# Projection with the first and second halves of all heads as two row tiles: rotary products without a rotation matmul

## The reference

```python
def rope(Y):                      # d = 16, so halves of 8
    ...
    Y2 = jnp.concatenate([-Y[..., d // 2:], Y[..., :d // 2]], axis=-1)
    return Y * cos + Y2 * sin     # cos, sin: the same 8 angles for both halves
q = split_heads(x @ Wq.T + bq); k = split_heads(x @ Wk.T + bk); v = split_heads(x @ Wv.T + bv)
q, k = (rope(q), rope(k))
att = softmax(causal(q k^T / sqrt(16)))
x = layernorm(x + (att @ v) @ Wo.T + bo)
x = layernorm(x + ffn(x))         # four ternary linear layers of width 1024, silu and gelu
```

## Time and profile before

| | |
|---|---|
| median of three runs | 2792.42 us (2791.34 to 2792.55) |
| profiled execution | 2795.36 us, span 2793.6 us |
| granted TensorE clock, mean | 0.989 of full |
| busy share of the span | PE 98%, DVE 68%, ACT 48%, POOL 5% |
| projection | 5.5 to 133.4 us of the span |

### The profile page before, as it was taken

The page is one execution under the profiler, slowest core; times in us unless marked ns, Lnnn a source line. Parts: engine busy times, 40 slices in busy tenths (PEclk is TensorE's granted clock), DMA queues, the critical chain, the costliest instruction groups (busy, mean ns, idle before and its releaser), DMA issues.

```text
span 2793.6 us, 39368 instructions
## 1 busy us (share of the span) xinstructions
PE 2729.1 (98%) x14880; PEld 1424.9 (51%) x14880; DVE 1899.9 (68%) x4003; ACT 1348.4 (48%) x2641; POOL 138.3 (5%) x206
## 2 busy tenths in 40 slices
PE   8899999999999999999999999999999999999998
PEld 4423333333333333333323333588888887888887
DVE  6999999888888888888887774633333352443343
ACT  4436666777776777777777776411111111000100
POOL 3300110001100001100000000000000000000000
PEclk9979999999999999999999999999999999999999
DMA  7731110001110011110001000411111132121100
GB/s 217 204 74 39 30 30 26 3 15 32 29 43 6 5 33 32 30 34 3 1 3 39 19 5 9 118 58 58 58 58 58 43 128 108 46 82 54 45 16 23
DMA packets 95613, 133.47 MB, mean 48 GB/s; under 512 B 31462, under 2 KB 69094, under 8 KB 91718
## 3 DMA queue, kind: packets, MB, share of 16 engines
q1 hardware_dynamic: 81452, 96.25, 10.7%
q0 software_dynamic: 6336, 23.34, 3.8%
q10 hardware_dynamic: 7648, 11.54, 1.5%
HBM read 83.77 MB, written 47.32 MB: 47 GB/s over the span
## 4 chain that ended last, share of the span: by engine, by line
PE 88%; DVE 6%; issue 2%; ACT 1%; DMA 1%; SPq 0%; ACTq 0%; POOLq 0%; POOL 0%; DVEq 0%
PE wi_f L984 19%; PE at_o L533 18%; PE at_row L498 17%; PE at_key L512 16%; PE na_h L1202 13%; PE na_y L1214 3%; DVE at_segmax L584 3%; DVE fr_masked L580 1%; DMA values<-pr_vals 1%; ACT at_probs L648 1%; PE at_key L515 1%; PE wi_p L833 1%; DVE pr_parts L252 0%; DVE pr_full L248 0%; PE pr_main L130 0%
## 5 line engine op out<-in xcount | busy, mean ns | idle before, releaser
L648 ACT ACTIVATE at_probs<-at_key 128x512 f32<-128x512 f32 (+3 forms) x2304 | 1127.3, 567 | 502.4 <-PE at_key L512 353.2
L584 DVE TENSOR_REDUCE at_segmax<-at_row 128x1 f32<-128x512 f32 x1792 | 1142.8, 684 | 169.2 <-PE at_row L498 164.9
L512 PE MATMUL at_key<-fr_q_stack,fr_k_stack 99*128 99x512 bf16 (+3 forms) x1152 | 415.0, 365 | 1.3 <-ACT at_probs L648 1.0
L498 PE MATMUL at_row<-fr_k_stack,fr_q_stack 96*128 96x512 bf16 (+3 forms) x1152 | 404.6, 376 | 10.8 <-DVE at_mask L612 5.5
L498 PE MATMUL at_row<-at_k_stack,at_q_stack 96*128 96x512 bf16 (+3 forms) x1152 | 408.1, 364 | 1.8 <-DVE at_segmax L584 1.1
L512 PE MATMUL at_key<-at_q_stack,at_k_stack 99*128 99x512 bf16 (+3 forms) x1152 | 402.2, 364 | 7.5 <-ACT at_probs L648 6.9
L1202 PE MATMUL na_h<-fr_h,fr_h2w_h 128*128 128x512 f32 x1024 | 322.1, 396 | 1.4 <-DVE fr_h L730 1.4
L533 PE MATMUL at_o<-at_probs,fr_values 128*32 128x512 f32 (+3 forms) x2304 | 289.0, 574 | 0.0
L533 PE MATMUL at_o<-at_probs,at_values 128*32 128x512 f32 (+3 forms) x2304 | 287.9, 572 | 0.0
L580 DVE CUSTOM_DVE_ANT_0 fr_masked<-at_row,fr_causal 128x384 f32<-128x384 f32 (+3 forms) x512 | 243.8, 483 | 45.1 <-PE at_row L498 44.7
L498 PEld LDWEIGHTS at_row<-fr_k_stack,fr_q_stack 96*128 96x128 bf16 x1152 | 110.3, 99 | 308.3 <-DVE at_segmax L584 160.1
(11 more groups left out here) (121 smaller groups left out, 2558.1 us busy)
## 6 DMA issues: line engine op xcount, KB each, us to landing
hidden<-wi_h SPq DMA_DIRECT2D x64, 256.0 KB, 2.0
na_h2f<-hidden SPq DMA_DIRECT2D x8, 1024.0 KB, 7.7
q_parts<-pr_parts SPq DMA_DIRECT2D x48, 128.0 KB, 2.4
k_parts<-pr_parts SPq DMA_DIRECT2D x48, 128.0 KB, 3.3
at_q_stack<-q_parts POOLq DMA_DIRECT2D x48, 128.0 KB, 3.5
at_k_stack<-k_parts POOLq DMA_DIRECT2D x48, 128.0 KB, 3.8
values<-pr_vals SPq DMA_DIRECT2D x32, 136.0 KB, 3.3
outputs<-at_outs SPq DMA_DIRECT2D x128, 34.0 KB
```

The costliest lines, as they stand in the source:

```text
L498: last = nc.tensor.matmul(bank[:, 0:w], qst[u][0:SROWS, c, h, i * P:(i + 1) * P], kst[u][0:SROWS, h, s * CH:s * CH + w], start=True, stop= ...
L512: last = nc.tensor.matmul(bank[:, q0:CH], kst[u][0:SROWS + PARTS, h, j * P:(j + 1) * P], qst[u][0:SROWS + PARTS, c, h, q0:CH], start=True, ...
L584: nc.vector.tensor_reduce(segmax[:, n % 2, h * TPC + i, s:s + 1], row_ps[r % RING_R][:, 0:w], op=ALU.max, axis=AX.X).then_inc(rows_taken, 1)
L648: nc.scalar.activation(probs[:, g % RING_P, h, q0:CH], key_ps[m % RING_K][:, q0:CH], ACT.Exp).then_inc(probs_ready, 1)
```

## The change

The rows of Wq and Wk and their biases are reordered on the way in: all first halves of the 16 heads (16 x 8 = 128 rows) are one tile, all second halves the other. A unit is now a **pair** of these tiles, q or k: g = 2n + m, 16 pairs. `rope` then works within partitions: full[first] = t1[first] - t2[second], full[second] = t1[second] + t2[first], with t2 = `lin` x sin. The matrix `turn`, `rotate` and `rot_ps` go. Four banks take the main products. Two `linear`, two POOL products and two sums are made per pair, 512 wide each; t2, rest, parts and ACT's two parts operations are made once per pair, 1024 wide. t2 reads `lin` in SBUF, where L237 read PSUM. The three parts of a half are stored by one DMA of 384 KB, so two DMAs a pair. `load_first` for the early chunks moves from ACT's queue to SP's, ahead of SP's wait for the parts. PE in `attend` waits for `consts_ready` only at the first turned row tile, and for `v_taken` only at the first keys; `t2_ready` isn't waited for any more.

```diff
-    UNITS = 2 * DH
-    NU = UNITS * NCH
+    PAIRS = 2
+    NU = PAIRS * NCH
     BUFS = 3
-    SLOTS = 4
+    SLOTS = 3
...
-            main(0)
             for g in range(NU):
-                if g + 1 < NU:
-                    main(g + 1)
-                rotate(g)
-                if g % 2 == 1:
-                    values(g // UNITS, g % UNITS // 2)
+                main(g)
+                values(*divmod(g, PAIRS))
...
+                m = g % PAIRS
+                for half in range(2):
+                    act.wait_ge(main_ready, 2 * g + half + 1)
+                    if g >= 2:
+                        act.wait_ge(t1_ready, 2 * (g - 2) + half + 1)
+                        act.wait_ge(t2_ready, g - 1)
+                    nc.scalar.activation(lin[:, g % 2, half, :], main_ps[2 * (g % 2) + half][:, :], ACT.Identity,
+                                         bias=bias[:, 2 * m + half:2 * m + half + 1],
+                                         scale=HD ** -0.5 if m == 0 else 1.0).then_inc(lin_ready, 1)
...
-                if 2 <= n < 2 + FIRST_EARLY:
-                    if m == 0:
-                        for slot in range(SLOTS):
-                            act.wait_ge(parts_stored[slot], 16 * PARTS * (n - 1))
-                    front.load_first(act, qp_d, kp_d, n - 2, range(m, len(TERMS), UNITS))
...
+                for half in range(2):
+                    pool.wait_ge(lin_ready, 2 * g + half + 1)
+                    if g >= 2:
+                        pool.wait_ge(full_ready, 2 * (g - 2) + half + 1)
+                    nc.gpsimd.tensor_tensor(t1[:, g % 2, half, :], lin[:, g % 2, half, :], cos[:, n % BUFS, :], ALU.mult
+                                            ).then_inc(t1_ready, 1)
...
-                    dve.wait_ge(rot_ready, g + 1)
-                    nc.vector.tensor_tensor(t2[:, g % 2, :], rot_ps[g % 2][:, :], sin[:, n % BUFS, :], ALU.mult
+                    dve.wait_ge(lin_ready, 2 * g + 2)
+                    if g >= 1:
+                        dve.wait_ge(full_ready, 2 * g)
+                    nc.vector.tensor_tensor(t2[:, :, :], lin[:, g % 2, :, :],
+                                            sin[:, n % BUFS, :].unsqueeze(1).broadcast_to([P, 2, CH]), ALU.mult
                                             ).then_inc(t2_ready, 1)
...
+                    for half, op in enumerate((ALU.subtract, ALU.add)):
+                        dve.wait_ge(t1_ready, 2 * g + half + 1)
+                        nc.vector.tensor_tensor(full[:, g % 2, half, :], t1[:, g % 2, half, :], t2[:, 1 - half, :], op
+                                                ).then_inc(full_ready, 1)
                 if 2 <= g:
                     dve.wait_ge(mid_ready, g - 1)
...
+                    nc.vector.tensor_tensor(parts[:, (g - 2) % SLOTS, 2, :, :], rest[:, (g - 2) % 2, :, :],
+                                            parts[:, (g - 2) % SLOTS, 1, :, :], ALU.subtract).then_inc(parts_ready, 1)
+                if g < NU:
+                    if g == 0:
                         dve.wait_ge(v_ones, 1)
                         dve.wait_ge(bv_loaded, 16)
-                    dve.wait_ge(v_ready, 2 * n + i + 1)
+                    dve.wait_ge(v_ready, g + 1)
                     if n > 0:
-                        dve.wait_ge(v_stored[i], 32 * n)
+                        dve.wait_ge(v_stored[m], 32 * n)
                     for j in range(2):
...
             for g in range(NU):
-                n, m = divmod(g, UNITS)
+                n, m = divmod(g, PAIRS)
+                early = n - 2
+                if 0 <= early < FIRST_EARLY:
+                    if m == 0:
+                        for slot in range(SLOTS):
+                            sp.wait_ge(parts_stored[slot], 16 * 2 * len(range(slot, PAIRS * (early + 1), SLOTS)))
+                    front.load_first(sp, qp_d, kp_d, early, range(m, len(TERMS), PAIRS))
                 sp.wait_ge(parts_ready, g + 1)
...
+                for half in range(2):
+                    sp.dma_start((qp_d, kp_d)[m].rearrange("a (p f) n t -> f p a n t", f=2)[half, :, :, n, :],
+                                 parts[:, g % SLOTS, :, half, :]).then_inc(parts_stored[g % SLOTS], 16)
+                sp.wait_ge(v_taken, g + 1)
+                for j in range(2):
+                    sp.dma_start(v_d[:, :, n, 2 * m + j, :].rearrange("q p e -> p q e"),
+                                 vals[:, m, j, :, :].rearrange("p (q h) e -> p q (h e)", q=NQUAD)
+                                 ).then_inc(v_stored[m], 16)
...
+                    if n == 0:
+                        pe.wait_ge(consts_ready, 2)
                     pe.wait_ge(maxparts_ready, n + 1)
...
-            pe.wait_ge(consts_ready, 2)
-            for name in ("lin_ready", "t2_ready", "v_taken"):
-                pe.wait_ge(*projected[name])
+            pe.wait_ge(*projected["lin_ready"])
```

More of the change, by code:

```diff
@@ L72, in project @@
         w = [sb(f"w{a}", [P, DH, D]) for a in "qkv"]
-        turn = sb("turn", [P, P])
-        bias = sb("bias", [P, UNITS])
+        bias = sb("bias", [P, 2 * PAIRS])
         bv = sb("bv", [P, D])
@@ L78, in project @@
         sin = sb("sin", [P, BUFS, CH])
-        lin = sb("lin", [P, 3, CH])
-        t1 = sb("t1", [P, 2, CH])
+        lin = sb("lin", [P, 2, 2, CH])
+        t1 = sb("t1", [P, 2, 2, CH])
         t2 = sb("t2", [P, 2, CH])
-        full = sb("full", [P, 2, CH])
-        rest = sb("rest", [P, 2, CH])
-        parts = sb("parts", [P, SLOTS, PARTS, CH], BF16)
+        full = sb("full", [P, 2, 2, CH])
+        rest = sb("rest", [P, 2, 2, CH])
+        parts = sb("parts", [P, SLOTS, PARTS, 2, CH], BF16)
         vals = sb("vals", [P, 2, 2, HEADS, VW])
-        main_ps = [ctx.enter_context(nc.psum_tensor(f"pr_main{i}", [P, CH], F32)) for i in range(3)]
-        rot_ps = [ctx.enter_context(nc.psum_tensor(f"pr_rot{i}", [P, CH], F32)) for i in range(2)]
+        main_ps = [ctx.enter_context(nc.psum_tensor(f"pr_main{i}", [P, CH], F32)) for i in range(4)]
         v_ps = [ctx.enter_context(nc.psum_tensor(f"pr_v{i}", [P, 2, D], F32)) for i in range(2)]
         w_loaded = [sem(f"w{a}_loaded") for a in "qkv"]
-        turn_loaded = sem("turn_loaded")
         bias_loaded = sem("bias_loaded")
@@ L100, in project @@
         lin_ready = sem("lin_ready")
-        rot_ready = sem("rot_ready")
         t1_ready = sem("t1_ready")
@@ L115, in load_weight, with load @@
             queue.dma_start(w[i][:, :, :], io[name].rearrange("(c p) o -> p c o", p=P)).then_inc(w_loaded[i], 16)
+        def load(queue, n):
+            u = n % BUFS
+            queue.dma_start(xt[:, u, :, :], io["xT"][n]).then_inc(x_loaded[u], 16)
+            queue.dma_start(cos[:, u, :], io["cos"][n]).then_inc(cos_loaded[u], 16)
+            queue.dma_start(sin[:, u, :], io["sin"][n]).then_inc(sin_loaded[u], 16)
         @block.tensor
@@ L119, in main @@
             def main(g):
-                n, m = divmod(g, UNITS)
+                n, m = divmod(g, PAIRS)
                 if m == 0:
                     pe.wait_ge(x_loaded[n % BUFS], 16 * (n // BUFS + 1))
[L124 to L141, removed]
+                if n == 0:
+                    pe.wait_ge(w_loaded[m], 16)
+                for half in range(2):
+                    if g >= 2:
+                        pe.wait_ge(lin_ready, 2 * (g - 2) + half + 1)
+                    bank = main_ps[2 * (g % 2) + half]
+                    for c in range(DH):
+                        last = nc.tensor.matmul(bank[:, :], w[m][:, c, half * P:(half + 1) * P], xt[:, n % BUFS, c, :],
+                                                start=(c == 0), stop=(c == DH - 1))
+                    last.then_inc(main_ready, 1)
             def values(n, i):
@@ L185, in _ @@
             for n in range(1, BUFS):
-                load(n)
+                load(act, n)
             act.wait_ge(bias_ready, 1)
@@ L250, in _ @@
                 if 2 <= g:
                     dve.wait_ge(mid_ready, g - 1)
-                    nc.vector.tensor_tensor(parts[:, (g - 2) % SLOTS, 2, :], rest[:, (g - 2) % 2, :],
-                                            parts[:, (g - 2) % SLOTS, 1, :], ALU.subtract).then_inc(parts_ready, 1)
-                if g < NU and m % 2 == 1:
-                    i = m // 2
-                    if g == 1:
+                    nc.vector.tensor_tensor(parts[:, (g - 2) % SLOTS, 2, :, :], rest[:, (g - 2) % 2, :, :],
+                                            parts[:, (g - 2) % SLOTS, 1, :, :], ALU.subtract).then_inc(parts_ready, 1)
@@ L1355, in shape_constants @@
     one = np.array([0x3F803F80], np.uint32).view(np.float32)[0]
-    turn = np.zeros((P, P), np.float32)
-    turn[p ^ (HD // 2), p] = np.where(p % HD < HD // 2, -1.0, 1.0)
     return dict(
         tables,
-        turn=turn,
         ones=np.full((PARTS, QUAD * T // 2), one, np.float32),
```

76 lines of the change are left out of this document (26 added, 50 removed).

## The result

The changed kernel takes 2866.53 us (median of four runs, 2864.71 to 2869.37) beside 2791.88 us of the kernel before (four runs, 2790.97 to 2792.55): ratio 1.0269, interval 1.0251 to 1.0286, thus +74.65 us. The forecast was 2858 us (+66), range 2828 to 2892.

A forecast was written before the change was run, and what follows sets the result against it. PE, with DVE nearly level, was taken to bound 96 to 124 us, ACT's issues and store waits to slow 44 to 96. Stage +64.5, late products +2, handover -0.5 gave +66: 2858 us, range 2828 to 2892.

The forecast's parts named there:

- The wait: DVE at `vals(g)` waits for values of pair g-2, issued behind parts(g-2): 14 waits, 5 to 9 us each.
- Its size: Store loop before `vals`: 9 waits of 6.3 us (middle of 4.7 to 7.8), 5 beside loads of 8.4; 98.7 us.
- Rival (c): Store loop: large DMAs land fast, waits about 4 us without loads, 6 with; 2825 us, chance 0.12.
- The ramp: Stage start before the waits: t2(1), a product in its way, ends 19.3, full(1) 21.6, full(2) 25.7, parts(0) 26.8 us.
- DVE's own work: DVE operations per pair, without waits or POOL's products: 5.25 us, before 5.46.
- late products: POOL's products reaching the next t2 when PE's clock falls: 0 to 14 us, taken as 2.
- The handover: Stage end: PE may start the rows before DVE's two casts, so DVE's 0.38 us wait goes: -0.5 us.
- Rival (d): DMA engines saturate (share 0.85): waits 11 us in six pairs with `load_first`, 7.8 in eight; 2888 to 2900 us, chance 0.15.
- load_first on SP: SP's queue: `load_first` goes out a period earlier, 0 us extra; ACT loses 36 issues and its 3.5 us stalls.
- Rival (a): Store loop costs little, DVE against POOL decides at 7.4 us per pair; 2786 us, or 2797; chance 0.05.
- Clock: PE, idle 6 to 7 us per pair, drops to clock 0.5 in parts; a pair then takes 10.3 us, below 12.

The follow-up runs named there:

- e1: Changed kernel, with SP issuing the values of pair g directly behind the parts of g-2: 2792.29 us, ratio 1.0000 to the kernel before.
- e2: Changed kernel with four buffers for `vals` instead of two, SP's order kept: 2793.93 us, ratio 1.0009 to the kernel before.
- e9: Kernel before, with SP issuing the values of unit u behind the parts of unit u+2: 2867.22 us, ratio 1.0271.
- e10: Changed kernel without ACT's five later loads of x, cos and sin: 2850.79 us, ratio 1.0213 to the kernel before.
- e7: e1 with the 36 `load_first` DMAs issued by ACT again instead of SP: 2787.57 us, ratio 0.9985 to the kernel before.
- e4: e1 with POOL's cosine products 64 columns wide instead of 512: 2775.97 us, ratio 0.9941 to the kernel before.
- e12: e11 with ACT doing `linear(g+2)` between its high and middle part, and t2 from PSUM: 2793.24 us, ratio 0.9997 to the kernel before.
- e13: e11 with ACT doing `linear(g+2)` between its high and middle part, t2 out of SBUF: 2788.22 us, ratio 0.999 to the kernel before.
- e11: e7 with four `parts` slots of a pair instead of three: 2784.79 us, ratio 0.9972 to the kernel before.

## Why the prediction was right

**The wait.** Right in place, number and consequence: 14 waits of `vals` for "DMA values", with ACT and POOL waiting behind. DVE's period is 11.1 to 12.2 us without a load (forecast 11 to 13) and 14.0 to 16.0 with one, more than forecast. e1 and e2 remove it by two ways and get back 74 and 73 us; e9 builds it into the old kernel and loses 75. This is shown.

**Its size.** The nine waits without a load: (103.8 - 48.2) / 9 = 6.2 us, forecast 6.3. The five with one (8.93, 10.52, 10.61, 9.46, 8.68): 9.6, forecast 8.4. Sum of waits 103.8 instead of 98.7, +5.1. The forecast's 2.1 us for a load, taken from one loop of the kernel before, measured 3.2 (e10): +5.7 in five pairs. That the rest came out is luck in part. The middle between 4.7 and 7.8 was chosen without a reason to prefer it, and two misses cancel in it: the plain loop is 5.9 us (e10), so 14 x 0.4 = 5 us less than forecast, and the six waits beside `load_first` are 0.7 us longer, 4 us that the forecast had at nothing. The parts of the loop were off as well: two parts issues and the first values issue take 0.89 + 0.9 = 1.8 us, not 1.4, and the values DMAs land 4.4 us after their issue in the median, not 3.3. Rival (c), S about 4, did not come: the shortest wait is 5.7.

**The ramp.** parts(0) ended at 30.7 and not at 26.8. The sums of pair 1 ended at 22.8, 1.2 late, since two products were in their way and not one; t2(2) took 0.4 more; and both products of pair 2 hit its sums, 2.14 more, which the term left out:

```profile
26.18 3.42 DVE L234 TENSOR_TENSOR pr_full<-pr_t 128x512 f32<-128x512 f32 x2
```

**DVE's own work.** 5.37 us a pair instead of 5.25: the 1024-wide operations come 1.14 apart, as forecast (1.13), the two sums take 1.20 as forecast; the rest is mainly that the parts operation runs its full 1.22 us before the wait, since nothing follows it at once. +1.6 us over the stage. With the three terms, 5.1 + 3.9 + 1.6 = 10.6, the forecast end of 197.9 becomes 208.5; measured 208.5. The 2 us for late products were not needed: beyond the ramp, products fell into the waits.

**The rest.** The median moved by 74.65 us and the end of the stage by 75.1. The two profiled executions lie 71.9 apart, since that of the kernel before was 3.5 us over its median and that of the changed one 0.7. The handover gave 0.38 us, forecast 0.5.

**Rival (d).** Its price did not come: the waits beside `load_first` are 6.3 to 6.9 us, and 9.5 to 10.6 with a load besides, not 11 in all six pairs, and those without either are 6.0 and not 7.8. As a mean the DMA share was 0.45 to 0.58 between 50 and 170 us, not 0.85. Its mechanism is there inside the waits, though, where the share is 0.91 with a load and 0.92 in the middle of a plain one. Loads cost more than forecast because they meet the stores in the one stretch in which DVE waits, and there the engines are nearly full.

**load_first on SP.** Forecast as free, since it would go out a period early. It goes out directly behind the values of the previous pair (SP's first issue of it is at 70.88 us, inside the wait that ends at 77.90), thus beside the very transfers that DVE waits for. The waits beside it are 0.6 to 0.7 us longer (e10); no run takes it out of the changed kernel. With the loop open it costs 4.7 us (e7). The prediction counted what is freed on ACT's queue and not what is then late on SP's; the DMA share of 0.85, which it took to agree, doesn't say what the choice of the queue costs.

**Rival (a).** Once the loop is open, DVE against POOL does decide, at the predicted 7.4 us a pair. The Trainium skill (SBUF — State Buffer, "Who interferes with whom") says that a DVE instruction with two SBUF inputs and a GpSimd instruction that reads SBUF shut each other out. e1 (1.07 us for each product), e4 (operations at 1.23 and 1.28 us once the products are cut) and the pair e12 and e13 agree. The 2786 us of that rival were reached only when load_first and the slots were mended as well (e11, 2784.79).

**Clock.** It fell as forecast, to 0.73 in 50 to 80 us and 0.60 in 170 to 205, and did not matter: PE, whose 8 values matmuls took 3.46 us where 1.89 stood before, still waits for DVE, and is not in the chain of 60 to 110 us.

```profile
78.71 3.46 PE L145 MATMUL pr_v<-pr_wv,pr_xt 128*128 128x256 f32 x8 [10.45 <-DVE pr_vals L248]
```

## What to carry to other kernels

Before fusing or re-skewing units, count for every reused buffer how many iterations lie between its release and its next use, and name the operation behind which the in-order queue issues the store that releases it; if this is the operation right in front of the waiting one, the whole store is on the path. The edit that mends it costs no time (issue stores in the order in which they are made, or give the small buffer two more copies, if there is room). Then look for the next limit before taking more work away: here these were GpSimd against DVE, `load_first` on the queue that stores, the slots of `parts`, and, not tested, the transfers themselves. Look at the DMA engines inside the waits and not over the stage: a mean share of 0.45 hid waits at 0.9.

## What was not expected of the hardware

- The issue of a values DMA took 0.9 us behind two 384 KB DMAs and 0.52 behind six of 128 KB: here the time on the issuing queue depended on what stood ahead of it.
- Six small DMAs instead of two large ones changed the time from parts to stored values by only 109.2 / 14 - 103.8 / 14 = 0.4 us.
- A GpSimd product costs DVE 1.07 us if it hits a 1024-wide operation (2.29 instead of 1.22), and two that hit two 512-wide ones cost the same each (3.42 instead of 1.28). Shorter DVE operations were no protection here. A product under a DVE operation with one operand in PSUM cost nothing (e12), under one with both in SBUF it waited (e13).
- With load_first on the queue that also stores, the stores come late: ACT waited 29.8 us for stored k parts in e1 and 17.3 in e7.
